# W1's stage and wo reordered, and the second adapter's product in three split instructions

## The chip, the cores and the metric

One core of a Trainium2 chip runs the whole kernel as one program. The metric is the time of one execution on the device in microseconds; before, the median of 3 runs is 2676.52 us (2675.76 to 2677.19).

## The reference

A transformer block on 32 sequences of 64 tokens, 2048 tokens of 1024 features in all, in fp32. Cut to what matters here:

```python
# first adapter (per sequence) and attention
c  = x @ W.T + b + 2.0 * (x @ A1[id]) @ B1[id]          # rank 16
o  = attention(rope(c @ wq), rope(c @ wk), c @ wv)      # 32 heads, 8 kv heads
x1 = x + o @ wo
# second adapter (8 experts, top 2, rank 16), then a routed FFN (16 experts, top 2, rank 64)
y  = x1 @ W2.T + 2.0 * sum_e gate_e * (x1 @ A2[e].T) @ B2[e].T
f  = y @ Wf.T + bf + 0.5 * sum_e comb_e * (y @ Af.T) @ Bf[e].T
out = x1 + f
```

The kernel multiplies Wf with W2 and with B2 at the start (the fold), so that the last stage needs x1 and two low-rank terms: the FFN's experts, 1024 rows, and the second adapter's 128 rows through the folded matrix c2 = Wf B2.

## The kernel before

The tokens go through in two halves (`hf`) of 1024, each as two column tiles `t` of 512. A wide product is 128 output rows by 512 tokens over 1024 inputs, in 8 chunks. Every factor of a wide product is split into a high part, rounded to TensorE's fp32r kind, and a low part, the rest; `three` (lines 646 to 648) then issues three instructions for each chunk: high by high, high by low, low by high. So a product is 24 instructions, and each operand needs a cast (ScalarE, `*_hi`) and a subtraction (GpSimd or VectorE, `*_lo`). Two low-rank products are left in plain fp32, one source instruction each: line 722, which adds the first adapter (b_rows by h_masked) to a product of W1, and line 1024, which adds the second (c_cols by h) to a product of the last stage. The trace shows each of them as two matmuls.

Every engine has its instructions in one written order, and each waits on counting semaphores. The stages, and what the change touches in them:

- Fold: 27 products in four PSUM banks; VectorE takes them (line 1487), and TensorE waited for the last take ahead of the loop over the halves.
- W1, of each half: tile 0 and tile 1 by the first 512 tokens, the small product h for the adapter, line 722 for both, then tile 2 with its line 722, and so on. h is masked on VectorE (line 1549) between pieces 0 to 3 and 4 to 7 of the split of x's second 512 tokens (xt_lo, line 1521). ScalarE casts tile 2, four pieces of x, tile 3, and four more. GpSimd subtracts W1's tiles (line 1367). SyncE issues, in this order: a wait for the output stores of the half before, eight b_rows loads with a register read ahead of each (lines 428 and 477), a wait for the products of the half before, eight x loads (line 441), then W1's tiles from 2 on (line 445).
- The quarters of wq, wk, wv with attention between them: not touched.
- wo, in four blocks of 1024 rows and eight tiles each: while a block is multiplied, the next block's o is cast on ScalarE and subtracted on GpSimd (line 1434), 16 pieces over the block's last four tiles.
- A stage of small products, with the routing.
- The last stage (s = 0 to 7, two products each): 24 instructions by the experts' rows, then line 1024. SyncE loads the next c_cols (line 627) when the product two tiles back is done, and the next half's x at s = 2. ScalarE casts the next weight tile, then issues the stores of the tile before, then casts x of the next half in s = 4 to 7. VectorE subtracts the next weight tile, takes the two products (line 1910) and then splits x.

TensorE writes into four banks in turn, so a product waits for the take of the fourth one before it.

Of the kernel before, what the change touches and what calls it, by code (L numbers as in the profile page):

```python
# [118 lines left out]
def build(nc, x, ids1, ids2, b1, A1, B1, wq, wk, wv, wo, W2, B2, Wf, bf, arf, wr2, tw, consts,  # L119
          gates_d, m_d, c2_d, o_d, ws_d, out):  # L120
    assert D == TOK and KC == TB
    with ExitStack() as ctx:
# [68 lines left out]
        OT = [sb(f"out_t{t}", [P, NT], offset=(184 + 2 * t) * KB) for t in range(TT)]  # L191
        BC = [sb(f"c2_cols{i}", [P, P], offset=(196 + i) * KB) for i in range(2)]

        RS = sb("rope_sin", [P, NT])
# [101 lines left out]
        step = sem("dve_step")  # L296
        logits_in = sem("logits_in")
        rexp = sem("route_exp")
        gates_in_sb = sem("gates_tok")
# [75 lines left out]
        def xt_no(hf, t, k):  # L375
            return (hf * TT + t) * KC + k + 1

        def fold_buf(i):

            return (i + 1) % 2  # L380
# [6 lines left out]
        def o_lo_at(hf, kb, i):  # L387

            return (hf * OKB + kb) * 16 - 4 * (hf + (kb > 0)) + i + 1

        def wo_q(kb, j, t):
# [4 lines left out]
        def _(sp):  # L396
# [161 lines left out]
            for hf in range(HALVES):  # L558
                q_base = qbase(hf)
                for t in range(TT):  # L560

                    sp.wait_ge(out_done[t], hf * (16 * KC) + 16)
                sp.wait_ge(fold_prod, 3 * (KC + 1))
                load_b1(hf, 0, slice(0, D))
                if hf:
                    sp.wait_ge(prod, q_base)
                load_x(hf, 1)
                for n in range(2, T_WO):
# [72 lines left out]
        def _(pe):  # L641
# [49 lines left out]


            pe.wait_ge(fold_taken, 3 * (KC + 1))

            for hf in range(HALVES):
# [37 lines left out]

                pe.wait_ge(xt_lo, xt_no(hf, 0, KC - 1))
                hold(pe)
                c_main(0)
                c_main(1)
                pe.wait_ge(a_lo, hf + 1)
# [271 lines left out]
                for s in range(KC):  # L1010
                    tile_ready(T_B + s)
                    for t in range(TT):
                        q = Q_O + TT * s + t
                        bank_free(q)

                        def g_chunk(k):
                            if s == 0 and t == 0:
                                pe.wait_ge(g_split, hf * KC + (k + 1))

                        main(q, s % 2, flat(XH, t), parts(XLP, t), stop=False, chunk=g_chunk)  # L1020
                        if t == 0:
                            pe.wait_ge(c2_in[s % 2], 16 * (hf * (KC // 2) + s // 2 + 1))
                            hold(pe)
                        pe.matmul(PJ[q % 4][:], BC[s % 2][:], H2[:, t * NT:(t + 1) * NT], start=False, stop=True  # L1024
                                  ).then_inc(prod, 1)


        @block.scalar
        def _(act):
# [52 lines left out]
            for hf in range(HALVES):  # L1082
# [190 lines left out]
                for kb in range(OKB):  # L1273
                    for j in range(KC):
                        n = kb * KC + j
                        for t in range(TT):
# [23 lines left out]
                            if t == TT - 1 and n + 2 < OKB * KC:  # L1300
                                tile_hi(hf, T_WO + n + 2, wo_q(kb, j, t))
                            if kb + 1 < OKB and j >= 4:
                                o_high(kb + 1, 4 * (j - 4) + 2 * t)
                                o_high(kb + 1, 4 * (j - 4) + 2 * t + 1)
                            if kb == OKB - 1 and j == KC - 2 and t == TT - 1:
# [36 lines left out]
                def store(s):  # L1342
                    for t in range(TT):
                        act.wait_ge(taken, q_base + (Q_O + TT * s + t + 1 + 4))
                        act.dma_start(out[hf * KC + s][:, t * NT:(t + 1) * NT], OT[t][:]).then_inc(out_done[t], 16)

                for s in range(KC):
                    if s < KC - 1:
                        tile_hi(hf, T_B + s + 1, Q_O - 1 if s == 0 else Q_O + TT * (s - 1) + 1)
                    if s:  # L1350
                        store(s - 1)
                    if hf + 1 < HALVES and s == KC - 1:
                        tile_hi(hf + 1, 0, Q_O + TT * (KC - 2) + 1 - Q_N)
                    if hf + 1 < HALVES and s >= 4:
                        x_hi(hf + 1, 0, 2 * (s - 4))
                        x_hi(hf + 1, 0, 2 * (s - 4) + 1)
                if hf + 1 < HALVES:
# [5 lines left out]
        def _(pool):  # L1363
# [6 lines left out]
            for hf in range(HALVES):  # L1370
# [71 lines left out]
                for kb in range(OKB):  # L1442
                    for j in range(KC):
                        n = kb * KC + j
                        if n + 2 < OKB * KC:
                            tile_lo(hf, T_WO + n + 2)
                        if kb + 1 < OKB and j >= 4:
                            for i in range(4):
                                o_low(kb + 1, 4 * (j - 4) + i)

# [11 lines left out]
        def _(dve):  # L1462
# [70 lines left out]
            for hf in range(HALVES):  # L1533
# [30 lines left out]

                for k in range(KC // 2):
                    x_lo(hf, 1, k)
                h_mask(0)
                for k in range(KC // 2, KC):
                    x_lo(hf, 1, k)
# [331 lines left out]
                dve.wait_ge(taken, q_base + (Q_O + 4))  # L1901

                for s in range(KC):
                    if s < KC - 1:
                        tile_lo(T_B + s + 1)
                    for t in range(TT):
                        q = Q_O + TT * s + t
# [3 lines left out]
                                          ALU.add).then_inc(taken, 1)  # L1911
                    if hf + 1 < HALVES and s >= 4:
                        x_lo(hf + 1, 0, 2 * (s - 4))
                        x_lo(hf + 1, 0, 2 * (s - 4) + 1)
                assert steps[0] == STEP_N, steps[0]
# [50 lines left out]
```

## Time and profile before

| | us |
|---|---|
| median of 3 runs | 2676.52 |
| the profiled execution | 2678.42 |
| its span, first to last instruction | 2676.6 |
| TensorE busy | 2617.3 |
| VectorE busy | 1325.4 |
| GpSimd busy | 1023.4 |
| ScalarE busy | 828.2 |

The profile is one execution; its views use one time axis, in microseconds from the first instruction. Busy TensorE is no bound by itself, because matmuls overlap: a matmul shown with 0.39 us follows the one before at a much shorter distance, and the distance is what counts. A wait is put down to the operation that released it last. "PEclk" is the clock that was granted to TensorE, 1.00 for 2.4 GHz and 0.50 for 1.2 GHz. The mean over the span was 0.992. The two halves run one after the other: the first begins after the fold, at about 125 us, the second at about 1400 us.

### The profile page before, as it was taken

Reading aid. Unit: us, or ns where it says so; the run is one execution under the profiler, and the core shown is the slowest. Engines: PE = TensorE matmul, PEld = TensorE weight load, DVE = VectorE, ACT = ScalarE, POOL = GpSimd, SP = SyncE. Lnnn points to the kernel's source line nnn. Section 1 sums busy time; section 2 is a strip of 40 time slices with the busy share of each in tenths; the row PEclk is TensorE's granted clock in tenths of the full one; section 3 lists DMA queues with packets and bytes.
Section 4 is the critical chain, followed back from the end, with each engine's and each line's share of the span. In section 5 each row is a group of like instructions: output and inputs, shape, how many; then the busy total and the mean of one; then the engine's idle time right before and its main releaser. Section 6 shows DMA issues by size and latency. Waiting matters only on the chain.

```text
span 2676.6 us, 35172 instructions
## 1 busy us (share of the span) xinstructions
PE 2617.3 (98%) x13416; PEld 2092.2 (78%) x13416; DVE 1325.4 (50%) x2017; ACT 828.2 (31%) x2048; POOL 1023.4 (38%) x670
## 2 busy tenths in 40 slices
PE   8989999999999999999998999999999999999999
PEld 7867777777776788888776787777777678888877
DVE  3236777777775111224522677777777511112451
ACT  2123344444444221211212334444444421121110
POOL 0025666666654433410202454333343443351030
PEclk9999999999999999999998999999999999999999
DMA  6332333333334513112442233333333452311332
GB/s 197 86 103 78 112 126 116 108 124 126 127 126 173 185 51 113 50 37 84 128 103 97 91 111 111 99 107 115 115 115 99 173 175 62 111 48 40 86 94 75
DMA packets 283064, 286.16 MB, mean 107 GB/s; under 512 B 47586, under 2 KB 225890, under 8 KB 282898
## 3 DMA queue, kind: packets, MB, share of 16 engines
q1 hardware_dynamic: 236034, 237.25, 28.0%
q10 hardware_dynamic: 46864, 46.67, 5.2%
q8 instruction: 108, 1.77, 0.3%
q14 instruction: 58, 0.48, 0.1%
HBM read 211.84 MB, written 72.02 MB: 106 GB/s over the span
## 4 chain that ended last, share of the span: by engine, by line
PE 90%; POOL 3%; DMA 3%; DVE 2%; SPq 1%; ACT 1%; issue 1%; POOLq 0%; ACTq 0%; DVEq 0%
PE prod L646 27%; PE prod L647 26%; PE prod L648 26%; PE turned L854 3%; PE turned L808 2%; POOL o_lo L1434 1%; PE prod L722 1%; PE prod L1024 1%; POOL s_lo L1387 1%; PE turned L823 1%; DMA raw<-in_wo 1%; PE prod L678 1%; DMA raw<-in_tw 1%; PE turned L838 0%; DVE xt_lo L1521 0%
## 5 line engine op out<-in xcount | busy, mean ns | idle before, releaser
L1367 POOL TENSOR_TENSOR w_lo<-raw,w_hi 128x1024 fp32r<-128x1024 f32 x96 | 239.1, 2491 | 816.3 <-ACT w_hi L1059 816.3
L646 PE MATMUL prod<-o_hi,w_hi 128*128 128x512 f32 x1024 | 403.1, 394 | 14.4 <-POOL o_lo L1434 10.3
L648 PE MATMUL prod<-o_hi,w_lo 128*128 128x512 f32 x1024 | 399.3, 390 | 0.0
L647 PE MATMUL prod<-o_lo,w_hi 128*128 128x512 f32 x1024 | 399.2, 390 | 0.0
L1725 DVE TENSOR_TENSOR x<-prod,x 128x512 f32<-128x512 f32 x128 | 88.5, 692 | 564.1 <-PE prod L648 564.1
L1387 POOL TENSOR_TENSOR s_lo<-w_sum,s_hi 128x512 fp32r<-128x512 f32 x192 | 249.6, 1306 | 298.8 <-ACT s_hi L1136 298.8
L1059 ACT CAST w_hi<-raw 128x1024 fp32r<-128x1024 f32 x130 | 136.2, 1048 | 689.3 <-PE prod L648 429.3
L646 PE MATMUL prod<-t_hi,s_hi 128*128 128x512 f32 x768 | 312.2, 407 | 6.8 <-POOL s_lo L1387 6.8
L647 PE MATMUL prod<-t_lo,s_hi 128*128 128x512 f32 x768 | 302.1, 393 | 0.0
L648 PE MATMUL prod<-t_hi,s_lo 128*128 128x512 f32 x768 | 301.8, 393 | 0.0
L1387 POOL TENSOR_TENSOR s_lo<-raw_pair,s_hi 128x512 fp32r<-128x512 f32 x144 | 198.8, 1388 | 149.9 <-ACT s_hi L1136 146.1
L646 PEld LDWEIGHTS prod<-o_hi,w_hi 128*128 128x128 f32 x1024 | 192.6, 188 | 66.1 <-POOL o_lo L1434 18.0
L1136 ACT CAST s_hi<-w_sum 128x512 fp32r<-128x512 f32 x192 | 116.4, 620 | 408.1 <-PE prod L648 328.8
L646 PE MATMUL prod<-b_hi,s_hi 128*128 128x512 f32 x576 | 232.6, 404 | 0.2 <-POOL s_lo L1387 0.2
L648 PE MATMUL prod<-b_hi,s_lo 128*128 128x512 f32 x576 | 224.8, 390 | 0.0
L647 PE MATMUL prod<-b_lo,s_hi 128*128 128x512 f32 x576 | 224.7, 390 | 0.0
L648 PEld LDWEIGHTS prod<-o_hi,w_lo 128*128 128x128 f32 x1024 | 192.5, 188 | 40.4
L647 PEld LDWEIGHTS prod<-o_lo,w_hi 128*128 128x128 f32 x1024 | 192.7, 188 | 38.6
L1612 DVE TENSOR_TENSOR rope_sin<-prod,consts_sb 64x512 f32<-64x512 f32 x320 | 220.3, 688 | 4.2
L646 PEld LDWEIGHTS prod<-t_hi,s_hi 128*128 128x128 f32 x768 | 145.3, 189 | 49.4 <-issue 17.7
L1168 ACT ACTIVATE probs<-probs,neg_max 128x64 f32<-128x64 f32 x512 | 170.8, 335 | 37.8 <-DVE neg_max L1638 37.8
L648 PEld LDWEIGHTS prod<-t_hi,s_lo 128*128 128x128 f32 x768 | 145.3, 189 | 31.4
(154 smaller groups left out, 4678.4 us busy)
## 6 DMA issues: line engine op xcount, KB each, us to landing
o_scratch<-o_out ACTq DMA_DIRECT2D x64, 512.0 KB, 3.1
raw<-in_wo SPq DMA_DIRECT2D x64, 512.0 KB, 4.0
o_raw<-o_scratch SPq DMA_DIRECT2D x64, 512.0 KB, 7.4
raw<-in_tw SPq DMA_DIRECT2D x50, 512.0 KB, 3.9
raw_pair<-in_wq SPq DMA_DIRECT2D x48, 512.0 KB, 3.7
w_sums_scratch<-w_sum SPq DMA_DIRECT2D x96, 256.0 KB, 4.4
w_sum<-w_sums_scratch SPq DMA_DIRECT2D x96, 256.0 KB, 4.5
xt_raw<-in_x SPq DMA_DIRECT2D x32, 256.0 KB, 5.5
```

The source lines that it names most:

```text
L646: pe.matmul(dst, wh, xh, start=start, stop=False)
L647: pe.matmul(dst, wh, xl, start=False, stop=False)
L648: return pe.matmul(dst, wl, xh, start=False, stop=stop)
L808: mm = pe.matmul(SCB[s * SEQ:(s + 1) * SEQ, o:o + SEQ], Q[r][t][:, c:c + SEQ], K[:, t * NT + c:t * NT + c + SEQ], start=True, stop=True)
L854: mm = pe.matmul(view(OB[b], GQ, s * SEQ, (s + 1) * SEQ), VV[rows, vv:vv + HD], pt[rows, hb, s], start=True, stop=True)
L1059: act.copy(WH[i % 2][:], RAW[i % 2][:]).then_inc(w_hi, 1)
L1136: act.copy(view(SH[i][:], 4), src).then_inc(s_hi, 1)
L1168: ins = act.activation(ss, ss, ACT.Exp, bias=NMX[:, r:r + 1], scale=SM_SCALE, accum_out=SUM[:, r:r + 1])
L1367: pool.tensor_tensor(WL[i % 2][:], RAW[i % 2][:], WH[i % 2][:].bitcast(F32), ALU.subtract).then_inc(w_lo, 1)
L1387: pool.tensor_tensor(view(SL[i][:], 4), src, view(SH[i][:].bitcast(F32), 4), ALU.subtract).then_inc(s_lo, 1)
L1612: ins = dve.tensor_tensor(view(RS[a:a + hd2, :], SPT), s3[b:b + hd2], sin, ALU.mult)
L1725: dve.tensor_tensor(X1[:, xs], PJ[q % 4][:], X1[:, xs], ALU.add).then_inc(taken, 1)
```

## The change

- SyncE: at the start of a half x is issued ahead of the wait for the output stores and of b_rows.
- TensorE: the wait for the last fold take moves behind the first W1 product; the first waits for one take less.
- VectorE: h is masked ahead of all eight pieces of x.
- wo: `o_parts` says which pieces of the next block are split at which product: in block 0 three at a time from tile 5 on, in blocks 1 and 2 two at a time as before.
- Last stage: h and each c_cols are cast on ScalarE and subtracted on VectorE (the low parts in the place of the fp32 data, the high parts in room that the stage before has done with), and line 1024 becomes a call of `three`. ScalarE casts the next c_cols ahead of the stores. The casts of the next half's x come one tile earlier, its subtractions ahead of the tile's takes.

```diff
@@ sync
-                for t in range(TT):
-
-                    sp.wait_ge(out_done[t], hf * (16 * KC) + 16)
                 sp.wait_ge(fold_prod, 3 * (KC + 1))
-                load_b1(hf, 0, slice(0, D))
                 if hf:
                     sp.wait_ge(prod, q_base)
                 load_x(hf, 1)
+                for t in range(TT):
+
+                    sp.wait_ge(out_done[t], hf * (16 * KC) + 16)
+                load_b1(hf, 0, slice(0, D))
@@ tensor
-            pe.wait_ge(fold_taken, 3 * (KC + 1))
...
                 pe.wait_ge(xt_lo, xt_no(hf, 0, KC - 1))
+
+                pe.wait_ge(fold_taken, 3 * (KC + 1) - 1)
                 hold(pe)
                 c_main(0)
+                pe.wait_ge(fold_taken, 3 * (KC + 1))
                 c_main(1)
...
                         if t == 0:
-                            pe.wait_ge(c2_in[s % 2], 16 * (hf * (KC // 2) + s // 2 + 1))
+                            pe.wait_ge(c2_lo, c2_no(hf, s))
                             hold(pe)
-                        pe.matmul(PJ[q % 4][:], BC[s % 2][:], H2[:, t * NT:(t + 1) * NT], start=False, stop=True
-                                  ).then_inc(prod, 1)
+                        ts = slice(t * NT, (t + 1) * NT)
+                        three(PJ[q % 4][:], BCH[s % 2][:], BCL[s % 2][:], H2H[:, ts], H2L[:, ts], False, True
+                              ).then_inc(prod, 1)
@@ scalar
-                            if kb + 1 < OKB and j >= 4:
-                                o_high(kb + 1, 4 * (j - 4) + 2 * t)
-                                o_high(kb + 1, 4 * (j - 4) + 2 * t + 1)
+                            for i in o_parts(kb, 2 * j + t):
+                                o_high(kb + 1, i)
...
+                def c2_high(s):
+                    act.wait_ge(c2_in[s % 2], 16 * (hf * (KC // 2) + s // 2 + 1))
+                    if s >= 2:
+                        act.wait_ge(prod, q_base + Q_O + TT * (s - 2) + TT)
+                    act.copy(BCH[s % 2][:], BC[s % 2][:]).then_inc(c2_hi, 1)
+
+
+                act.wait_ge(prod, q_base + Q_O)
+                act.copy(H2H[:], H2[:]).then_inc(c2_hi, 1)
+                c2_high(0)
                 for s in range(KC):
                     if s < KC - 1:
                         tile_hi(hf, T_B + s + 1, Q_O - 1 if s == 0 else Q_O + TT * (s - 1) + 1)
+                    if s < KC - 1:
+                        c2_high(s + 1)
                     if s:
                         store(s - 1)
...
-                    if hf + 1 < HALVES and s >= 4:
-                        x_hi(hf + 1, 0, 2 * (s - 4))
...
+                    if hf + 1 < HALVES and 3 <= s < 7:
+                        x_hi(hf + 1, 0, 2 * (s - 3))
@@ vector
-                for k in range(KC // 2):
-                    x_lo(hf, 1, k)
                 h_mask(0)
-                for k in range(KC // 2, KC):
+                for k in range(KC):
                     x_lo(hf, 1, k)
...
+                def c2_low(s):
+                    dve.wait_ge(c2_hi, c2_no(hf, s))
+                    dve.tensor_tensor(BCL[s % 2][:], BC[s % 2][:], BCH[s % 2][:].bitcast(F32), ALU.subtract
+                                      ).then_inc(c2_lo, 1)
+
+                dve.wait_ge(c2_hi, c2_no(hf, -1))
+                dve.tensor_tensor(H2L[:], H2[:], H2H[:].bitcast(F32), ALU.subtract).then_inc(c2_lo, 1)
+                c2_low(0)
                 for s in range(KC):
                     if s < KC - 1:
                         tile_lo(T_B + s + 1)
+                        c2_low(s + 1)
+                    if hf + 1 < HALVES and s >= 4:
+                        x_lo(hf + 1, 0, 2 * (s - 4))
+                        x_lo(hf + 1, 0, 2 * (s - 4) + 1)
                     for t in range(TT):
...
```

The new helper, used by ScalarE's `o_high` and GpSimd's `o_low`:

```diff
+        def o_parts(kb, m):
+            if kb + 1 == OKB:
+                return range(0)
+            if kb == 0:
+                return range(3 * (m - 10), min(3 * (m - 9), 16)) if m >= 10 else range(0)
+            return range(2 * (m - 8), 2 * (m - 7)) if m >= 8 else range(0)
```

## Rows read from the trace of the kernel before

**Rows 1.** The page, chain that ended last: share of the span by engine.
```profile
PE 90%; POOL 3%; DMA 3%; DVE 2%; SPq 1%; ACT 1%; issue 1%; POOLq 0%; ACTq 0%; DVEq 0%
```

**Rows 2.** Waits of TensorE, whole span: who for whom, total us, times, longest.
```profile
PE prod L722 <- DVE h_masked L1549: 19.0, 2, 10.9
...
PE prod L646 <- DVE xt_lo L1521: 4.4, 1, 4.4
...
PE prod L646 <- POOL w_lo L1367: 4.1, 2, 2.5
```

**Rows 3.** The chain, 120 to 160 us: start us, length us, what.
```profile
124.78 0.27 SPq L428
...
134.13 0.36 SPq L441
...
137.86 6.53 DMA raw<-in_tw
...
153.21 3.75 PE prod L722 x4
```

**Rows 4.** The chain, 1395 to 1440 us.
```profile
1399.82 0.70 DVE out_t L1910
...
1402.67 0.27 SPq L428
...
1411.38 0.42 SPq L441
...
1415.17 7.62 DMA raw<-in_tw
...
1431.58 3.75 PE prod L722 x4
```

**Rows 5.** Timeline of TensorE where the halves start: start us, us, instruction, idle before.
```profile
125.72 0.47 PE L646 MATMUL prod<-xt_hi,w_hi 128*128 128x512 f32 x1 [1.03 <-DVE m_rows L1487]
...
162.48 1.02 PE L722 MATMUL prod<-h_masked,b_rows 128*128 128x512 f32 x2
...
1398.76 1.02 PE L1024 MATMUL prod<-h,c_cols 128*128 128x512 f32 x2
...
1441.58 1.02 PE L722 MATMUL prod<-h_masked,b_rows 128*128 128x512 f32 x2
```

**Rows 6.** Busy by stretch: PE, PEld, DVE, ACT, POOL, granted clock, DMA, GB/s.
```profile
1404.20:1409.90 5.70, 5.70 (x14) 4.44 (x15) 1.90 (x1) 0.00 (x0) 0.00 (x0) 0.50 0.21 64
```

**Rows 7.** DMA issues by line: KB each, median us to landing.
```profile
raw<-in_tw SPq DMA_DIRECT2D x50, 512.0 KB, 3.9
...
b_rows<-in_B SPq DMA_DIRECT2D x16, 64.0 KB, 2.0
...
c_cols<-c_scratch SPq DMA_DIRECT2D x16, 64.0 KB, 1.9
```

**Rows 8.** Timeline of GpSimd, 118 to 175 us.
```profile
145.61 2.35 POOL L1367 TENSOR_TENSOR w_lo<-raw,w_hi 128x1024 fp32r<-128x1024 f32 x1 [16.15 <-ACT w_hi L1059]
```

**Rows 9.** Timeline of VectorE, 118 to 175 us.
```profile
146.09 6.38 DVE L1521 TENSOR_TENSOR xt_lo<-xt_raw,xt_hi 128x512 fp32r<-128x512 f32 x4 [14.48 <-ACT xt_hi L1052]
152.39 0.68 DVE L1549 TENSOR_TENSOR h_masked<-prod,consts_sb 128x512 f32<-128x512 f32 x1
152.99 2.48 DVE L1521 TENSOR_TENSOR xt_lo<-xt_raw,xt_hi 128x512 fp32r<-128x512 f32 x4
```

**Rows 10.** Timeline of all engines, 1290 to 1335 us.
```profile
1298.12 0.39 PE L646 MATMUL prod<-x_hi,w_hi 128*128 128x512 f32 x1
...
1298.37 1.05 ACT L1059 CAST w_hi<-raw 128x1024 fp32r<-128x1024 f32 x1 [5.85 <-PE prod L648]
...
1299.73 1.22 DVE L1741 TENSOR_TENSOR w_lo<-raw,w_hi 128x1024 fp32r<-128x1024 f32 x1
...
1303.56 1.02 PE L1024 MATMUL prod<-h,c_cols 128*128 128x512 f32 x2
```

**Rows 11.** The chain, 860 to 960 us.
```profile
885.79 11.96 DMA raw<-in_wo
```

More of the change, by code:

```diff
@@ L192, in build @@
         BC = [sb(f"c2_cols{i}", [P, P], offset=(196 + i) * KB) for i in range(2)]
+        BCL = [sb(f"c2_lo{i}", [P, P], F32R, offset=(196 + i) * KB) for i in range(2)]
+        BCH = [sb(f"c2_hi{i}", [P, P], F32R, offset=(4 + i) * KB) for i in range(2)]
+        H2H = sb("h2_hi", [P, TOK], F32R, offset=0)
+        H2L = sb("h2_lo", [P, TOK], F32R, offset=192 * KB)
         RS = sb("rope_sin", [P, NT])
@@ L297, in build @@
         logits_in = sem("logits_in")
+        c2_hi = sem("c2_hi")
+        c2_lo = sem("c2_lo")
         rexp = sem("route_exp")
@@ L376, in xt_no, with c2_no @@
             return (hf * TT + t) * KC + k + 1
+        def c2_no(hf, s):
+            return hf * (KC + 1) + s + 2
         def fold_buf(i):
@@ L1353, in _ @@
                         tile_hi(hf + 1, 0, Q_O + TT * (KC - 2) + 1 - Q_N)
-                    if hf + 1 < HALVES and s >= 4:
-                        x_hi(hf + 1, 0, 2 * (s - 4))
-                        x_hi(hf + 1, 0, 2 * (s - 4) + 1)
+                    if hf + 1 < HALVES and 3 <= s < 7:
+                        x_hi(hf + 1, 0, 2 * (s - 3))
+                        x_hi(hf + 1, 0, 2 * (s - 3) + 1)
                 if hf + 1 < HALVES:
@@ L1446, in _ @@
                             tile_lo(hf, T_WO + n + 2)
-                        if kb + 1 < OKB and j >= 4:
-                            for i in range(4):
-                                o_low(kb + 1, 4 * (j - 4) + i)
+                        for i in (*o_parts(kb, 2 * j), *o_parts(kb, 2 * j + 1)):
+                            o_low(kb + 1, i)
                 pool.wait_ge(w_hi, tile_no(hf, T_AR) + 1)
@@ L1911, in _ @@
                                           ALU.add).then_inc(taken, 1)
-                    if hf + 1 < HALVES and s >= 4:
-                        x_lo(hf + 1, 0, 2 * (s - 4))
-                        x_lo(hf + 1, 0, 2 * (s - 4) + 1)
                 assert steps[0] == STEP_N, steps[0]
```

## The prediction

> **What bounds the kernel now.** I read the chain of waits first: nine tenths of the span is TensorE at work [rows 1], so time comes back only where TensorE idles or where its own instructions get shorter. The list of what TensorE waits for comes next [rows 2]. Its longest entry is the first adapter's product (line 722), which waits 19.0 us for h_masked in two places, one per half (10.9 and so 8.1); behind it stand 4.4 us for xt_lo and 4.1 us for w_lo. The chain around these two places shows what h_masked itself waits for. In half 0 SyncE wakes at 124.78, issues eight b_rows loads until 134.13, eight x loads until 137.86, and only then W1's tile 2, which takes 6.53 us to land behind the x traffic; ScalarE casts that tile before it casts x, VectorE subtracts four x pieces before it masks h, and TensorE starts line 722 at 153.21 [rows 3]. In half 1 the queue starts later still: the last product of half 0 is taken at 1399.82, the b_rows loads wait for the last output store (1402.67), x follows at 1411.38, the tile at 1415.17 with 7.62 us to land, line 722 at 1431.58 [rows 4]. To measure all of a half's start in one number I use the start of the product of tile 2 with line 722, because it contains every stall and slow instruction before it: 162.48 and 1441.58 [rows 5]. After the 4.4 us wait the granted clock is 0.50 (the 1.2 GHz level) over 1404.20 to 1409.90, and 14 matmuls take 5.70 us [rows 6].
>
> **The start of a half.** Three edits belong together: SyncE issues x before b_rows, VectorE masks h before any piece of x, and x of the next half's first tile is split before the last outputs are taken. In half 0 the two groups of loads cost 3.73 and 9.35 us of SyncE in either order [rows 3], so tile 2 is still issued at 137.86. But x is then issued from 124.78 on and out of its way, so I give the tile the 3.9 us that such a load takes in the median [rows 7]: 141.76. From landing to GpSimd's start now takes 145.61 - (137.86 + 6.53) = 1.22 us, the subtraction 2.35 [rows 3, 8], and from VectorE's mask to TensorE it is 153.21 - (152.39 + 0.68) = 0.14 [rows 3, 9], which I take for this step too: tile 2 can start at 145.47. TensorE itself is there earlier. It no longer holds its first product for the last fold bank (it starts at 125.72 today, 1.03 us of it that wait [rows 5]); from 124.78, 72 instructions at 0.2267 us (worked out below) end at 141.1, the mask's 0.68 and the 0.14 [rows 9] follow, and b_rows, issued by 137.86 with 2.0 to land [rows 7], is in; two adapter products at 0.907 end at 143.7. So the wait on h_masked shrinks to 0.8, a wait on w_lo of 1.8 takes its place, and the earlier start of TensorE is worth nothing by itself. Tile 2's 24 instructions then take 5.44, and line 722 comes at 150.91 instead of 162.48: **11.6 us**.
>
> In half 1 x can be issued from 1399.82, 3.79 us of it, until 1403.61, by when the stores are in (1402.67); b_rows takes 8.71, until 1412.32 [rows 4]; then 3.9, 1.22, 2.35 and 0.14 as before give 1419.93. TensorE starts at once, since xt_lo was done before the last takes: 72 instructions, the mask and two adapter products end at 1399.82 + 16.3 + 0.8 + 1.8 = 1418.7, so again the tile is last, by 1.2. Line 722 comes at 1425.37 instead of 1441.58: **16.2 us**. The 4.4 us wait on xt_lo and the slow clock behind it [rows 2, 6] are inside this number and are not added.
>
> What this adds: all eight x pieces now follow the mask on VectorE and stand beside GpSimd's subtractions of tiles 2 and 3. Four pieces took 6.38 us there and 2.48 when GpSimd was idle [rows 9]; from about 143 the eight end at the latest at 143 + 12.8 = 155.8, and the first to need them is the second h product, after tile 3, at 145.47 + 2 x (5.44 + 0.907) = 158.2. Two microseconds of cover; without it TensorE would wait for xt_lo there, one for one.
>
> In these rows VectorE loses by the neighbourhood (1.6 us a piece against 0.62) and GpSimd's subtraction of tile 2 does not (2.35) [rows 8, 9]; ScalarE casts tile 2 before x, so GpSimd starts first, in the new order too, and I charge nothing. Were a piece of x to come first and GpSimd to wait for it, tile 2, now the last arrival, would come later by up to a piece, 0.62, in each half: 1.2 us off the sum. The Trainium skill speaks for such a wait: its page "SBUF — State Buffer", section "SBUF: two separate sides", says that VectorE and GpSimd share a port pair, held for a whole instruction by whichever starts first while the other is fully blocked; the trace agrees as far as VectorE's 1.6 us go, and shows no case of the other side.
>
> **The second adapter's product (line 1024).** 24 instructions of the split kind last from 1298.12 to 1303.56, 0.2267 each [rows 10]. Products begin (1398.76 - 1303.56)/15 = 6.347 apart [rows 5, 10], so the fp32 product costs 6.347 - 5.440 = 0.907, four times a split instruction. Three split ones cost 0.680. 32 products x 0.227 = **7.3 us**, all on the path, as TensorE never waits in this stage. No row shows three split instructions of other operands at the end of a group. A loss is excluded, as is a larger gain, because every one of the 24 before them keeps this pitch; the other end is no gain, if changing operands costs the three what the fp32 product costs. I take 7.3, since those 24 are the nearest row.
>
> The split itself is paid on ScalarE and VectorE. At the stage's start ScalarE casts h (1.05, from 1298.37), VectorE, free at 1299.73, subtracts (1.22) [rows 10]: 1300.95. The 128x128 columns have no row; between nothing and these 1.05 and 1.22 for eight times the elements, I take 0.3 each. Even at the upper end c2_lo stands at 1302.2 and TensorE asks at 1303.56: 1.4 us of cover, which TensorE's own 24 instructions give. Tile 1's subtraction slips to 1304.6 at most and is needed at 1310. Later columns are issued when tile s-1 is done and needed 2 x 6.12 + 5.44 = 17.7 us on; landing 1.9 [rows 7], a cast and a subtraction are 4.2 at most. Behind the columns' cast on ScalarE, which waits for their landing, now stand the output stores of tile s-1 and the x casts, some 2 us later, and VectorE's next take waits for a store; four banks give TensorE about 18 us before it would notice. The x pieces before the takes cost VectorE 1.3 of the same cover. All zero.
>
> **wo.** The high and low parts of block 1 move from tile 4 to tiles 5 to 7. TensorE's wait for w_lo here (4.1 in two places) ends with a wo load that lands 11.96 us after its issue, behind the o loads [rows 2, 11], and SyncE's order there is unchanged: zero. Between a gain of 4.1 and a loss of one GpSimd subtraction per half, 2 x 2.35 [rows 8]; I take zero because the load's row is the nearest; both ends lie in the range.
>
> **The sum.** 11.6 + 16.2 + 7.3 = 35.1 us. The profiled execution took 2678.42 (span 2676.6 and 1.8 around it); it becomes 2643.3. The median of the runs, 2676.52, is 1.9 below it: **2641.4**.
>
> **The rivals.** (a) Tile 2 lands as slowly as today, or the clock falls in the new gaps. With 6.53 and 7.62 instead of 3.9 the sum loses 2.6 and 3.7; a stretch at the low clock as in rows 6 would lose 5.70 - 14 x 0.2267 = 2.5 per half. The gain is then 28.8 or 30.1, the time 2647.7 or 2646.4. For it: tile 3 is issued right behind; against: the last x load is issued nine microseconds before, and the gaps are 0.8 to 1.8. (b) Tile 2 lands early and TensorE's own path is the bound: another 1.8 and 1.2, 2638.4. (c) The split product does not get cheaper, so that the change does there not what it says: 27.8 alone, 2648.7. Against it speaks that the same triple runs at 0.2267 everywhere. (d) A piece of x holds up GpSimd's subtraction of tile 2 in both halves: 1.2 less, 2642.6; against it stands the order of the casts. (e) The other side: slower. The split product waits, in order on TensorE, for c2_lo, and the whole stage is behind it; c2_lo hangs on a DMA, ScalarE and VectorE in turn. Slack is 17.7 - 4.2 = 13.5 us for 14 tiles (seven in each half). To eat 35.1 each would have to be 2.5 late, which means columns landing in about 18 us instead of 1.9; at 19 us it would be 2690. Only the x loads of the next half share the queue at one tile, so I see little for it.
>
> **How the numbers follow.** Forecast 0.66; (a) 0.12; (b) 0.08; (c) 0.05; (d) 0.04; (e) and other ways to lose 0.05, of which 0.03 slower and 0.02 within 0.2% (5.4 us, about what a measurement of this kernel can tell from no change). The range reaches from (b) with one microsecond to spare to (a) and (c): 2637 to 2650. Faster 0.95, same 0.02, slower 0.03.
>
> **What would show it.** Right: h_masked falls to under 2 us in TensorE's waits and w_lo appears after it with 1 to 2 us in each half; the xt_lo wait is gone; tile 2's line 722 stands some 26 us after the last fold product; products in the last stage are 6.12 apart, with no wait on c2_lo. Wrong: a wait on c2_lo or xt_lo of several microseconds, a clock of 0.50 after the mask, tile 2 landing in more than 6 us, or products still 6.3 apart.

## The result, and the profile after

| | before | after |
|---|---|---|
| median, us | 2676.14 (2675.11 to 2677.19, 4 runs) | 2645.26 (2644.01 to 2647.44, 4 runs) |
| the profiled execution | 2678.42 | 2646.27 |
| its span | 2676.6 | 2644.5 |
| mean granted clock | 0.992 | 0.997 |

The ratio is 0.9885, with a 95% interval of 0.9869 to 0.99: 30.9 us less by the medians, 32.15 by the two profiled executions. Forecast were 35.1. The time lies inside the range, 3.9 above the forecast and 1.1 below the 2646.4 of the second branch of rival (a).

What TensorE waits for, after the change (who for whom, total us, times, longest), answers to [rows 2]:

```profile
PE prod L665 <- POOL w_lo L1398: 8.7, 4, 2.7
...
PE prod L697 <- DMA raw<-in_W: 6.5, 1, 6.5
PE prod L738 <- DVE h_masked L1579: 1.9, 2, 0.9
```

Line 722 is now line 738, and its 19.0 us for the mask are 1.9. The wait of 4.4 for xt_lo is gone. In their place w_lo has two more waits, 2.73 and 2.59, one per half. The chain (start us, length us, what) shows where tile 2's time comes from. Half 0, which answers to [rows 3]:

```profile
125.00 1.20 SPq L460
126.25 0.94 SPq L460
...
130.02 0.28 SPq L447
...
139.07 3.75 DMA raw<-in_tw
```

and half 1, which answers to [rows 4]:

```profile
1387.90 0.70 DVE out_t L1950
1388.62 4.85 DMA out<-out_t
1393.55 0.27 SPq L447
...
1402.44 3.53 DMA raw<-in_tw
```

The last output store of the kernel before, from the view of [rows 4], which do not show this line:

```profile
1400.54 2.07 DMA out<-out_t
```

The tile lands in 3.75 and 3.53 us, as forecast (3.9). But the second and third x loads take 1.20 and 0.94 us of SyncE to issue, and in half 1 the last output store takes 4.85 us where it took 2.07, with the x loads beside it; b_rows waits for that store.

TensorE's timeline (start us, us, instruction, the wait before it in brackets) answers to [rows 5]:

```profile
141.86 1.95 PE L738 MATMUL prod<-h_masked,b_rows 128*128 128x512 f32 x4 [0.95 <-DVE h_masked L1579]
146.54 0.47 PE L665 MATMUL prod<-xt_hi,w_hi 128*128 128x512 f32 x1 [2.73 <-POOL w_lo L1398]
...
153.71 0.59 PE L738 MATMUL prod<-h_masked,b_rows 128*128 128x512 f32 x1
...
1409.67 0.47 PE L665 MATMUL prod<-xt_hi,w_hi 128*128 128x512 f32 x1 [2.59 <-POOL w_lo L1398]
...
1416.81 0.59 PE L738 MATMUL prod<-h_masked,b_rows 128*128 128x512 f32 x1
```

Line 738 of tile 2 stands at 153.71 instead of 162.48. In half 1 it comes 28.9 us after the last product of half 0 is taken, where it came 41.8 after. Tile 2's own 24 instructions last 153.71 - 146.54 = 7.17 and 7.14 instead of 5.44, and the view by stretch says why (us, then busy time and count of PE, PEld, DVE, ACT, POOL, then the granted clock, the share of DMA, GB/s; answers to [rows 6]):

```profile
147.20:150.70 3.50, 3.50 (x10) 2.72 (x9) 3.50 (x3) 3.03 (x6) 2.59 (x1) 0.52 0.43 150
1410.10:1413.50 3.40, 3.40 (x10) 2.63 (x9) 3.40 (x3) 3.25 (x7) 2.72 (x1) 0.50 0.56 154
```

Right behind either wait for w_lo the clock is at the level of 1.2 GHz.

The last stage, TensorE at s = 6 of half 0, and the new preparation by groups (busy us, mean ns):

```profile
1368.66 0.39 PE L665 MATMUL prod<-h_hi,c_hi 128*128 128x512 f32 x1
...
1374.78 0.39 PE L665 MATMUL prod<-h_hi,c_hi 128*128 128x512 f32 x1
```

```profile
L1370 ACT CAST c_hi<-c_cols 128x128 fp32r<-128x128 f32 x16 | 4.7, 297 | 8.7 <-DMA c_cols<-c_scratch 8.7
...
L1933 DVE TENSOR_TENSOR c_lo<-c_cols,c_hi 128x128 fp32r<-128x128 f32 x16 | 4.5, 284 | 0.0
```

Products are 6.12 apart, and no wait on c2_lo is in the list. The cast and the subtraction of the columns take 0.30 and 0.28 us; 0.3 each was the estimate.

Stage by stage the two profiled executions differ so:

| stage | forecast | measured |
|---|---|---|
| start of half 0, to line 738 of tile 2 | 11.6 | 8.77 |
| start of half 1, counted from the last take of half 0 | 16.2 | 12.85 |
| last stages, both | 7.3 | 7.16 |
| quarters and wo | 0 | 1.35 + 2.45 - 0.4 = 3.4 |

The terms of the last line are half 1's quarters, half 1's wo, and half 0's quarters, which are 0.4 longer. It is not the change's, as the repeated runs show further down; without it the profiles give 28.8 us.

### The profile page after: what moved, and what is told of

The parts are those of the page before. It is cut to its first block, busy times and chain, and to the rows that moved or that the text cites. A ratio compares the mean times of both kernels' runs of the same rounds, so it can differ in the third digit from the quotient of the medians.

```text
span 2644.5 us, 35285 instructions
## 1 busy us (share of the span) xinstructions
PE 2602.4 (98%) x13448; PEld 2094.4 (79%) x13448; DVE 1338.2 (51%) x2035; ACT 833.9 (32%) x2066; POOL 1023.3 (39%) x670
## 4 chain that ended last, share of the span: by engine, by line
PE 90%; POOL 4%; DMA 2%; DVE 1%; SPq 1%; ACT 1%; issue 1%; POOLq 0%; ACTq 0%; DVEq 0%
PE prod L665 28%; PE prod L667 27%; PE prod L666 27%; PE turned L873 3%; PE turned L827 2%; POOL o_lo L1465 1%; POOL s_lo L1418 1%; PE turned L842 1%; PE prod L738 1%; DMA raw<-in_wo 1%; PE prod L697 1%; PE turned L857 0%; DMA raw_pair<-in_wq 0%; POOL w_lo L1398 0%; ACT probs L1188 0%
```

## The experiments

Times are medians; each run's ratio is to the kernel before on the same chip, 2676.1 to 2676.6 in all of them.

**The split product alone.** The kernel after with all of the reordering undone, that is, these lines as before, wo and the casts of the next x too:

```diff
+                for t in range(TT):
+
+                    sp.wait_ge(out_done[t], hf * (16 * KC) + 16)
                 sp.wait_ge(fold_prod, 3 * (KC + 1))
+                load_b1(hf, 0, slice(0, D))
                 if hf:
                     sp.wait_ge(prod, q_base)
                 load_x(hf, 1)
-                for t in range(TT):
-
-                    sp.wait_ge(out_done[t], hf * (16 * KC) + 16)
-                load_b1(hf, 0, slice(0, D))
...
+                for k in range(KC // 2):
+                    x_lo(hf, 1, k)
                 h_mask(0)
-                for k in range(KC):
+                for k in range(KC // 2, KC):
                     x_lo(hf, 1, k)
```

> The kernel before with the split of the second adapter's product alone (casts, subtractions, three instructions). My theory: 32 products, each 0.227 us shorter, so 7.3 us less than before, 2668.9; products of the last stage 6.12 apart, nothing else moved. Rival: the split also changes the starts of the halves (ScalarE's and VectorE's extra work ahead of the second half), then it is off by several microseconds, and the second half's line 722 of tile 2 no longer comes 41.8 us after the last product of the first half.

2669.99 us (2668.69 to 2672.35, 11 runs), ratio 0.9979 (0.997 to 0.9988): 6.2 less than before, against 7.3. The waits are those of before, with h_masked at 19.9 and w_lo at 3.3 instead of 4.1. Line 738 of tile 2 comes 41.2 us after the last take of half 0, against 41.8 before, so the rival falls. From the second adapter's first product to the last take, a last stage takes 92.68 us in either half of this profile and of every other profile with the split, and 96.26 in every profile without it: 7.2 for both. So the product pays alone, and about what was worked out.

**All but the split product.** The kernel after with the fp32 product back, and without the casts and subtractions for it:

```diff
-                        three(PJ[q % 4][:], BCH[s % 2][:], BCL[s % 2][:], H2H[:, ts], H2L[:, ts], False, True
-                              ).then_inc(prod, 1)
+                        pe.matmul(PJ[q % 4][:], BC[s % 2][:], H2[:, t * NT:(t + 1) * NT], start=False, stop=True
+                                  ).then_inc(prod, 1)
```

> The changed kernel with the fp32 product of the second adapter back, all of the reordering kept. My theory: the parts add up, so 7.3 us more than the changed kernel, about 2652.5; tile 2's line 722 at 153.7 and 28.9 us after the last product of half 0, as in the changed kernel. Rival: the split's work on ScalarE delays the stores and with them b_rows in half 1 (the last store landed 5.7 us after the last product); then here the store lands in about 3 us, b_rows starts earlier, and the second half gains 1 to 2 us more.

2652.66 us (2646.96 to 2656.78, 5 runs), ratio 0.9914 (0.9901 to 0.9928): 7.4 above the kernel after. Its TensorE timeline at the start of half 0 and in the last stage, and the stretch behind the wait:

```profile
146.40 0.47 PE L665 MATMUL prod<-xt_hi,w_hi 128*128 128x512 f32 x1 [2.84 <-POOL w_lo L1392]
...
1367.82 1.02 PE L1043 MATMUL prod<-h,c_cols 128*128 128x512 f32 x2
...
1374.17 1.02 PE L1043 MATMUL prod<-h,c_cols 128*128 128x512 f32 x2
```

```profile
146.00:150.00 4.00, 3.60 (x16) 3.00 (x17) 4.00 (x3) 4.00 (x7) 2.98 (x2) 1.00 0.41 131
```

The products are 6.35 apart again. The gap before tile 2 is as long as in the kernel after, 2.84 (2.61 in half 1), and here the clock stayed at 2.4 GHz behind it in both halves: such a gap is not always followed by the low clock. Up to half 0's tile 2 the two kernels have the same instructions, so it is not the edit that decides there. The rival falls: the last store of half 0 lands in 4.79 us, as in the kernel after, and the 1.5 us that this start of half 1 is shorter are the clock. This profile is of the shortest of the five runs (2646.96), and its kernel's runs spread over 10 us; that it is only 0.7 above the profile of the kernel after, with last stages 7.2 longer, is due to fewer stretches of low clock and shorter waits.

**wo alone.** The kernel before with `o_parts` in the two places where ScalarE and GpSimd take the pieces of the next block.

```diff
-                            if kb + 1 < OKB and j >= 4:
-                                o_high(kb + 1, 4 * (j - 4) + 2 * t)
-                                o_high(kb + 1, 4 * (j - 4) + 2 * t + 1)
+                            for i in o_parts(kb, 2 * j + t):
+                                o_high(kb + 1, i)
```

> The kernel before with the new places of the o pieces in wo alone. My theory: nothing, 2676 within 1 us; TensorE still waits 1.6 and about 2.5 us for w_lo in wo, because a wo load that stands behind the o loads ends it. Rival: the 2.4 us that half 1's wo gained in the changed kernel come from this edit; then 2673.7, and the wait for w_lo in half 1 falls to about 1.7.

2676.06 us (11 runs), ratio 1.0 (0.9991 to 1.0009). Nothing in the time, as forecast. The wait for w_lo in half 1's wo is 0.34 us in this profile, where some 2.5 was expected. It is no mark of the edit: with wo as before it is 2.52 in the profile of the kernel before and 1.70 in that of the first experiment, with the new places 0.34 here and 1.68 in the kernel after.

**SyncE's order undone.** The kernel after with b_rows ahead of x again (the first hunk of the first experiment alone).

> The kernel after with one part undone: SyncE issues b_rows ahead of the eight x loads again (the mask's piece stays first on VectorE and the product stays split). My theory: the x loads ahead of b_rows are what let W1's tile 2 land in 3.5 to 3.75 us; with them behind, tile 2 shares the queues with them again and lands 6.5 us (half 0) and 7.6 us (half 1) after its issue, as in the kernel before. Against the kernel after that makes tile 2 about 1.6 us later in half 0 and 4.9 us in half 1 (there the store of the last product also lands in about 2.1 us again instead of 4.85, which is taken off already): about 2651.8 us. Rival: what counted was the mask alone, and a tile that lands later only takes up the wait of 2.7 us that TensorE has anyway: within 0.5 us of the kernel after, 2645 us.

2652.01 us (2650.41 to 2658.08, 4 runs), ratio 0.9907 (0.9892 to 0.9922): 6.75 above the kernel after, and the rival, no difference, falls. The profile is of the longest of its four executions, 6 us above their median. Its waits and, from its chain, the loads:

```profile
PE prod L665 <- POOL w_lo L1398: 15.9, 4, 7.4
```

```profile
139.21 7.34 DMA raw<-in_tw
...
1393.28 2.07 DMA out<-out_t
1408.31 7.17 DMA raw<-in_tw
```

Tile 2 lands in 7.34 and 7.17 us when the x loads are issued right ahead of it. The store of the last product lands in 2.07 when no x load is issued beside it, and the eight x loads then take 3.77 us to issue (5.29 in half 0 of the kernel after). The mechanism is the one expected, and the median meets the 2651.8. In this profile TensorE begins tile 2 2.4 us later in half 0 and 4.9 in half 1 than in the kernel after, where 1.6 and 4.9 were worked out; with a longer stretch of low clock behind the wait the two starts are 3.0 and 6.0 longer.

**The mask behind four pieces of x.** The kernel after with VectorE's order undone (the second hunk of the first experiment alone).

> The kernel after with another part undone: VectorE makes four pieces of x in bf16 ahead of the half's mask, as before the change. My theory: those four pieces run beside GpSimd's remainder of tile 2 at about 1.6 us each, so the mask, and with it the two products on line 738, come about 5 us later in each half: a wait of line 738 on h_masked of about 5 us in the waits, and a time of about 2655 us. Rival: the pieces now find their x loads landed before tile 2 and run at 0.6 us each ahead of GpSimd's remainder, and the mask is late by only some 2.5 us a half, half of which falls into the wait on w_lo: about 2647.5 us.

2663.12 us (2662.91 to 2664.3, 5 runs), ratio 0.9953 (0.9939 to 0.9966): 17.9 above the kernel after. Both theories had too little. The waits, and VectorE and ScalarE of this kernel in half 0:

```profile
PE prod L738 <- DVE h_masked L1579: 21.0, 2, 10.8
```

```profile
144.77 6.38 DVE L1551 TENSOR_TENSOR xt_lo<-xt_raw,xt_hi 128x512 fp32r<-128x512 f32 x4 [12.48 <-ACT xt_hi L1072]
151.08 0.68 DVE L1579 TENSOR_TENSOR h_masked<-prod,consts_sb 128x512 f32<-128x512 f32 x1
```

```profile
143.18 1.04 ACT L1079 CAST w_hi<-raw 128x1024 fp32r<-128x1024 f32 x1 [13.71 <-DMA raw<-in_tw]
144.13 2.17 ACT L1072 CAST xt_hi<-xt_raw 128x512 fp32r<-128x512 f32 x4
```

I had counted only the 6.38 us of the four pieces. VectorE stands idle for 12.48 before them, because ScalarE casts x behind tile 2, and tile 2 is the load that SyncE issues last. In VectorE's order the mask is thus behind a DMA that it has no need of. It comes at 151.08 instead of 141.02, with its product done since 142. (The pieces are fp32r, as everywhere; "bf16" in the expectation is a slip.)

**The gap filled.** The kernel after with ten matmuls, whose result nothing uses, between line 738's pair and tile 2:

```diff
                 c_lora(1)
+                for i in range(10):
+                    pe.matmul(TP[0][:, 0:NT], AH[:, 0:P], XTH[0][:, 0:NT], start=True, stop=True)
                 for n in range(2, T_WO):
```

> The changed kernel with ten matmuls more in each half, on operands that are there and into a bank that nobody reads, between the two products of line 722 and tile 2, where TensorE waits 2.7 and 2.6 us for w_lo. They take 2.3 us and so fit in the wait. My theory: the clock falls after that wait because TensorE stood still; filled, the granted clock stays 1.00 over tile 2, whose 24 instructions then take 5.5 us instead of 7.1, and 3.3 us come back: 2642. Rival: tile 2's instructions are slow there because x is being cast and subtracted beside them; then they are slow here too and the time is that of the changed kernel, 2645.

2644.95 us (2644.03 to 2645.89, 4 runs), ratio 0.9882 (0.9867 to 0.9897). Its TensorE timeline and the stretch:

```profile
144.49 2.84 PE L766 MATMUL turned<-xt_hi,lora_a_hi 128*128 128x512 f32 x10
147.69 0.47 PE L665 MATMUL prod<-xt_hi,w_hi 128*128 128x512 f32 x1 [0.35 <-POOL w_lo L1400]
...
153.25 1.02 PE L738 MATMUL prod<-h_masked,b_rows 128*128 128x512 f32 x2
```

```profile
146.00:152.00 6.00, 5.65 (x25) 4.34 (x25) 6.00 (x4) 5.33 (x10) 4.34 (x2) 1.00 0.28 89
```

With the gap filled the clock holds, and tile 2 takes 5.56 instead of 7.17, with x cast and subtracted beside it as before; in half 1 the clock holds as well. On the spot the theory is right and the rival falls: beside the kernel after, 1.7 us are won in half 0 and 1.0 in half 1. Yet the time is the rival's, only 0.3 shorter than the kernel after. The two traces say where the rest is: W1 begins 1.2 later, behind the first wait for in_W at the kernel's start, and a stretch at the low clock at about 1513, in the quarters, costs 1.3 that the first profile of the kernel after does not have. Whether either belongs to the edit is a question for the repeated runs.

**W1's tiles 2 and 3 ahead of b_rows.**

```diff
                 load_x(hf, 1)
+                load_w1(hf, 2)
+                load_w1(hf, 3)
                 for t in range(TT):
                     sp.wait_ge(out_done[t], hf * (16 * KC) + 16)
                 load_b1(hf, 0, slice(0, D))
-                for n in range(2, T_WO):
+                for n in range(4, T_WO):
```

> The kernel after with W1's tiles 2 and 3 issued right behind the x loads, ahead of SyncE's wait for the stores and of b_rows. My theory: the 2.6 to 2.7 us that TensorE still waits for w_lo in each half is the price of tile 2 standing behind the stores and b_rows, and the low clock behind it comes from that gap. Then both go: 2.7 + 1.7 us in half 0 and 2.6 + 1.7 us in half 1, so 8.7 us off, about 2636.5 us, and the waits name w_lo only for wo (1.5 to 2 us). Rival: b_rows is then the last to arrive (it has two tiles of W1 ahead of it in the queue), the mask comes 2 to 3 us later and line 738 waits for it as long as TensorE waited for w_lo: 2644 to 2646 us, with h_masked at 5 to 7 us in the waits.

2640.0 us (2639.55 to 2640.47, 4 runs), ratio 0.9864 (0.9849 to 0.9879): 5.3 less than the kernel after. Its waits:

```profile
PE prod L667 <- POOL w_lo L1400: 3.1, 2, 1.6
...
PE prod L740 <- DMA b_rows<-in_B: 1.1, 1, 1.1
PE prod L740 <- DVE h_masked L1581: 0.9, 1, 0.9
```

and a stretch at tile 2 in half 0, and one in half 1's quarters:

```profile
141.90:150.00 8.10, 7.15 (x29) 5.19 (x29) 7.85 (x11) 3.15 (x6) 2.13 (x1) 1.00 0.43 129
...
1507.30:1510.50 3.20, 3.20 (x9) 2.46 (x9) 3.10 (x5) 0.19 (x1) 3.20 (x4) 0.50 0.00 0
```

The waits on w_lo at the halves' starts are gone, and no low clock follows. Line 740 of tile 2 comes 4.6 earlier in half 0, counted from W1's first product, and 4.3 in half 1, counted from the last take: 8.9, where 8.7 was expected. The rival's bound is there, but small: in half 1 b_rows comes 1.1 late. The 3.6 us by which the medians show less are 1.1 at the kernel's start, 1.3 at 1507, 0.5 in half 0's quarters, and 1.0 by which the median of the kernel after lies below its profiled execution, from whose trace I had worked; 0.3 comes back elsewhere.

**Tile 2's product ahead of line 738 as well.** The kernel of the last experiment, and TensorE's order changed:

```diff
                 h_lora(0)
+                c_main(2)
                 pe.wait_ge(taken, q_base + QN["h0"] + 1 + 4)
...
-                    c_main(n)
+                    if n > 2:
+                        c_main(n)
```

> The kernel with tiles 2 and 3 first, and besides TensorE runs tile 2's product ahead of the two products of line 738 on tiles 0 and 1, so that the mask has 5.4 us more. My theory: the two waits of 0.9 us for the mask go too: about 2634.7 us, and no wait on h_masked is left. The rival of the run with the tiles first (mask late by 2 to 3 us) would show here as no wait either, since 5.4 us cover it: also about 2635 us, so that the two runs together tell whether the mask became the bound. A third way: tile 2's product now comes 1.8 us earlier and w_lo is late for it by that much: no gain over the run with the tiles first.

2636.63 us (2634.49 to 2640.69, 4 runs), ratio 0.9855 (0.984 to 0.987). No wait for the mask or for b_rows is left in its list, and three products of line 738 (line 740 here) follow each other without one:

```profile
146.56 2.74 PE L740 MATMUL prod<-h_masked,b_rows 128*128 128x512 f32 x6
```

**The last two questions: what repeats.** The same kernel, and the kernel after, run once more on one chip.

> The kernel with tiles 2 and 3 first and tile 2's product ahead of line 738's, once more beside the kernel after on one chip. My theory: the 8.7 us of the waits for w_lo and of the low clock behind them and the 1.8 us of the waits for the mask are gone for good: 2634 to 2638 us, 8 to 10.5 us under the kernel after. Rival: its first four runs (2634.5 to 2640.7) were a mixture, and it is no better than the kernel with the tiles first alone: 2640 us.

2636.47 us (2635.23 to 2637.21, 5 runs), ratio 0.9848 (0.9834 to 0.9861): it beats the kernel after, by 8.8 us against the first measurement of that. All five lie below the rival's 2640, which falls so far; but the kernel with the tiles first was not run on this chip, and the intervals of the two ratios overlap (0.9849 to 0.9879 there), so what the order adds is known less well than the whole.

> The kernel after itself, once more, to see what a second profile of the same program changes. My theory: the stages around the change repeat within 0.5 us (line 738 of tile 2 some 11 to 12 us after the third wait for in_W is taken out, waits on w_lo of 8 to 9 us), while the first wait for in_W (6.5 us in the first profile, 7.1 to 8.4 in the experiments) and the stretches of low clock away from the half starts (one of 1.35 us in half 1's quads in five other profiles, none there in the first of this kernel) differ by 1 to 2 us and are not the change's: a time of 2645 to 2647.5 us. Rival: those 1.35 us and the 2.45 us of half 1's wo belong to the change, and the second profile has no low clock there either: 2644 to 2646 us.

Three executions of 2645.95, 2647.47 and 2652.61 us; a fourth took 7685.84, for which nothing on record gives a cause, and the ratio leaves it out. Ratio 0.9887 (0.9869 to 0.9905). The profile is of the longest. Two stretches of it, in wo of half 0 and of half 1, and under them two of the kernel before, in half 1's quarters and wo:

```profile
895.50:898.90 3.40, 3.40 (x10) 2.66 (x9) 0.00 (x0) 2.00 (x4) 3.40 (x3) 0.50 0.72 215
2151.60:2155.00 3.40, 3.40 (x10) 2.62 (x9) 0.00 (x0) 2.61 (x6) 3.40 (x3) 0.50 0.61 179
```

```profile
1539.70:1543.00 3.30, 3.30 (x9) 2.53 (x8) 3.21 (x6) 0.00 (x0) 3.30 (x4) 0.50 0.00 0
2174.50:2177.90 3.40, 3.40 (x10) 2.63 (x9) 0.00 (x0) 1.37 (x3) 3.40 (x3) 0.50 0.50 144
```

The first profile of the kernel after has neither of the first two; the second loses 2.0 and 2.2 us there. So low clock in wo comes and goes with the execution, and the 2.45 us that half 1's wo seemed to win belong to no edit. It does not come from nowhere: in the twelve profiles the four stretches of low clock in wo follow TensorE's four longest waits for w_lo there (1.90, 1.98, 2.30 and 2.52 us), and behind the other twenty, none over 1.71, there is none.

At about 1510 the second profile has no low clock either. Here the kernel of the last two experiments, with tile 2's product ahead of line 738, settles it. There are two profiles of it too, and this is the same place in its quarters, behind a wait of 2.36 us in both:

```profile
1502.40:1505.80 3.40, 3.40 (x9) 2.63 (x8) 3.13 (x5) 0.66 (x2) 3.40 (x3) 0.50 0.00 0
```

```profile
1505.10:1508.50 3.40, 3.40 (x15) 2.54 (x14) 3.13 (x5) 0.67 (x2) 3.40 (x3) 1.00 0.00 0
```

One program, the low clock in one execution and not in the other, and half 1's quarters differ by 1.37 us: so the 1.35 in the quarters is no mark of an edit either. The same goes for the kernel's start: W1's first product comes 0.8 later in the second profile of the kernel after than in the first.

The start of half 0 repeats within 0.1 us, counted from that product. In half 1 the last store lands in 5.96 instead of 4.85, b_rows waits for it, and w_lo's wait is 3.6: this start alone is worth 1.1 us more or less. One of the three executions, 2652.61, lies above the 2647.5 that I expected at most.

## Why the prediction was right, and where its sizes were off

**What bounds the kernel.** Right: the gain came from the two starts and the last stage, and wo alone gave nothing. Undone one at a time, the mask costs 17.9, SyncE's order 6.75, the split product 7.4, together 32.05 against 30.9 for the whole change. The sum is no proof that the parts add: the first two act on the same starts, and costs of one edit undone at a time need not add. Two edits have no run of their own, the casts and subtractions of x that took the 4.4 us wait for xt_lo away, and the later wait for the last fold take; what they are worth by themselves is not shown.

**The mask.** Right, with the size: a wait of 0.8 was forecast on h_masked and 0.95 is there. A wait on w_lo behind it was forecast with 1 to 2, and it is 2.7 and 2.6. So tile 2 is the last arrival, as the forecast had it, and rival (b), TensorE's own path as the bound, is out. But two of the signs were missed: this wait is longer than it was to be, and line 738 of tile 2 stands some 29 us behind the last fold product, not 26. And one of the signs of being wrong, a clock of 0.50 after the mask, is there in both halves. The next two paragraphs say what that was.

**Tile 2's issue.** The gain from this term was put too high. I let SyncE's two groups of loads take the same 3.73 and 9.35 us in either order. x takes 5.4 where it now stands, and tile 2 is issued at 139.07, not 137.86: 1.2 us. The fold's last store is issued in the same stretch (125.36); that it is the cause was not tried. In half 1 I let the stores be in at 1402.67, their time of before. With the x loads beside it the last store lands 2.8 later; b_rows starts 5.65 after the last take instead of 3.8, and the tile is issued 2.0 late. The fourth experiment shows both prices: with x behind, 3.77 and 2.07. The tile's landing was right, and gives back 0.15 and 0.4.

**The clock.** This was rival (a), second branch, with 0.12: the clock falls in the new gap. It did in both profiles of the kernel after, in both halves. Its price was 2.5 a half and is 1.7. I set it aside because the gap was to be 0.8 to 1.8; the gap became 2.7 by the term above. The filled gap shows that the 1.7 go when TensorE has work there; the kernel without the split shows gaps of the same length with the clock at 1.00. What decides between them I cannot tell from these runs.

So half 0 lacks 1.2 - 0.15 + 1.7 = 2.8 and half 1 lacks 2.0 - 0.4 + 1.7 = 3.3, which is all of 11.6 - 8.8 and of 16.2 - 12.9. That the time came out only 3.9 above the forecast is in part luck: the change's own stages give 28.8 us, and the 3.4 us in the quarters and wo (2.1 of the 30.9 by the medians) hid part of the shortfall.

**The x pieces beside GpSimd.** The timelines of VectorE and of GpSimd answer to [rows 8, 9]:

```profile
141.02 0.69 DVE L1579 TENSOR_TENSOR h_masked<-prod,consts_sb 128x512 f32<-128x512 f32 x1 [9.52 <-PE prod L667]
144.52 8.83 DVE L1551 TENSOR_TENSOR xt_lo<-xt_raw,xt_hi 128x512 fp32r<-128x512 f32 x8 [2.80 <-ACT xt_hi L1072]
```

```profile
144.04 2.35 POOL L1398 TENSOR_TENSOR w_lo<-raw,w_hi 128x1024 fp32r<-128x1024 f32 x1 [14.69 <-ACT w_hi L1079]
147.07 2.72 POOL L1398 TENSOR_TENSOR w_lo<-raw,w_hi 128x1024 fp32r<-128x1024 f32 x1 [0.67 <-ACT w_hi L1079]
```

The first three of the eight pieces one by one, and GpSimd's subtraction of tile 3 in the kernel before:

```profile
144.52 2.43 DVE L1551 TENSOR_TENSOR xt_lo<-xt_raw,xt_hi 128x512 fp32r<-128x512 f32 x1 [2.80 <-ACT xt_hi L1072]
146.87 0.68 DVE L1551 TENSOR_TENSOR xt_lo<-xt_raw,xt_hi 128x512 fp32r<-128x512 f32 x1
147.47 2.86 DVE L1551 TENSOR_TENSOR xt_lo<-xt_raw,xt_hi 128x512 fp32r<-128x512 f32 x1
```

```profile
148.63 2.68 POOL L1367 TENSOR_TENSOR w_lo<-raw,w_hi 128x1024 fp32r<-128x1024 f32 x1 [0.68 <-ACT w_hi L1059]
```

Right in its result: eight pieces took 8.83 us against the bound of 12.8, no wait for xt_lo came, and GpSimd's subtraction of tile 2 lasted 2.35, as before, with VectorE's pieces from 0.5 us after its start. Rival (d) is not seen for tile 2. But the reading behind it was wrong. The 1.6 us a piece are a mean of two kinds: a piece that begins while GpSimd subtracts takes 2.4 to 2.9 and ends 0.55 us after GpSimd does (146.95 against 146.40, 150.33 against 149.79), and all others take 0.68. That is why the eight pieces lose 3.9 us (8.83 against twice 2.48), no more than the four did (6.38 against 2.48). And the kernel before did have a case of the other side: its subtraction of tile 3, at 148.63, began 0.2 us into a piece of VectorE and took 2.68, and the one at 147.07 here began 0.2 us into one and took 2.72, both 0.3 to 0.4 more than the 2.35 of one that began first. It cost nothing, since TensorE takes up tile 3 at 154.73 without a wait. The Trainium skill's rule ("SBUF — State Buffer", "SBUF: two separate sides"), by which the one that starts second is blocked until the other is done, agrees with both.

**The split product.** Right: 0.227 saved for each, no wait on c2_lo, the columns' cast and subtraction 0.30 and 0.28. Rivals (c) and (e) are out: the products stand 6.12 apart.

## What to carry to other kernels

An engine's order can tie an operation to a load that it has no need of. The mask's product was done some nine microseconds before; four pieces ahead of it in VectorE's order waited for a cast that ScalarE had queued behind a weight tile. So follow each entry ahead of the late one to its own releaser, and on that engine to the entry before it.

When transfers are moved, price them anew where they then stand: the same eight loads cost 3.7 or 5.3 us to issue, and the store that they now ran beside took 2.8 us longer and held up the queue. And when one wait is removed, issue what is late next ahead of what has slack: two weight tiles issued ahead of b_rows, and TensorE's order changed so that it uses the first of them before the late product, gave another 8.8 us.

## What the runs showed of the hardware

- A store of 256 KB landed in 2.07 us with no loads beside it (the kernel before and two runs), and in 4.79 to 5.96 beside eight loads of 256 KB (five profiles).
- After a gap of 2.6 to 3.7 us TensorE's clock was at 1.2 GHz over the first matmuls of tile 2 in both halves of two profiles; after gaps of 2.84 and 2.61 us it was not, in a kernel that differs only in its last stage.
- Single stretches at the low clock lie in the quarters and in wo in some executions of a program and not in others, at 1.3 to 2.2 us each, waits included, and each follows a wait of TensorE. A difference of 2 us between two profiles of this kernel is therefore no evidence for an edit before the stretch that holds it is found.
- A VectorE piece of x that began while GpSimd subtracted a weight tile ended 0.55 us after GpSimd did, in all nine cases in the profiles of the kernel before and after, and took 2.4 to 2.9 us where a piece alone took 0.68. A GpSimd subtraction that began 0.2 us into such a piece took 2.67 to 2.72 us, one that began first 2.35.
